# Spreading the attention row factors of a four-layer graph network by VectorE block transposes and DMA instead of TensorE transposes

## What is computed

```
x = layernorm(x + L0(x))      # 4 heads of 32: softmax(mask(q k^T / sqrt(32))) v, then @ wo.T + bo
x = layernorm(x + L1(x))      # h = x W; e[n,m] = leaky_relu(s1[n] + s2[m]); softmax over masked m; @ h
x = layernorm(x + L2(x))      # the same with 8 heads of 16 and a prior, then @ W_out.T
x = layernorm(x + L3(x))      # MLP, attention without mask, elu, MLP, masked attention, elu, residuals
```

## Time and profile before

| | us |
|---|---|
| median of 3 runs | 1141.66 |
| lowest, highest | 1140.52, 1142.09 |
| the profiled execution's own time | 1140.98 |
| its span, from the first to the last instruction | 1139.2 |
| PE busy (share of the span) | 1045.3 (92%) |
| DVE busy | 917.0 (80%) |
| ACT busy | 736.3 (65%) |
| POOL busy | 271.4 (24%) |

### The profile page before, as it was taken

The page is one execution under the profiler, slowest core; times in us unless marked ns, Lnnn a source line. Parts: engine busy times, 40 slices in busy tenths (PEclk is TensorE's granted clock), DMA queues, the critical chain, the costliest instruction groups (busy, mean ns, idle before and its releaser), DMA issues. The chain is left out here.

```text
span 1139.2 us, 26405 instructions
## 1 busy us (share of the span) xinstructions
PE 1045.3 (92%) x9333; PEld 782.5 (69%) x9333; DVE 917.0 (80%) x2514; ACT 736.3 (65%) x1901; POOL 271.4 (24%) x381
## 2 busy tenths in 40 slices
PE   2899999999999999999999999999999999879763
PEld 1567676877677767777787867777787768555552
DVE  4467999989897988979797997989797997977342
ACT  1699577757677684867678584867678584533522
POOL 0012212213131231413132141313132131421212
PEclk9999999999999999999999999999999999999877
DMA  4000000000000000000000000000000000000000
GB/s 120 1 11 12 11 2 11 1 11 11 10 2 12 10 11 11 11 11 11 11 2 11 10 11 11 11 11 11 11 1 11 2 11 2 10 1 10 10 0 19
DMA packets 9489, 12.97 MB, mean 11 GB/s; under 512 B 2704, under 2 KB 5008, under 8 KB 9232
## 3 DMA queue, kind: packets, MB, share of 16 engines
q1 hardware_dynamic: 9360, 11.28, 3.3%
HBM read 7.08 MB, written 4.19 MB: 10 GB/s over the span
## 5 line engine op out<-in xcount | busy, mean ns | idle before, releaser
L1119 DVE SCALAR_TENSOR_TENSOR P<-bank,t2e,mask_t 128x512 f32<-128x512 f32 x512 | 344.8, 739 | 19.1 <-PE bank L561 19.0
L703 ACT ACTIVATE probs<-probs,neg_max 128x512 f32<-128x512 f32 x256 | 184.8, 724 | 9.5 <-DVE neg_max L949 8.0
L748 ACT ACTIVATE x<-x,shift_l,rstd_l 128x128 f32<-128x128 f32 x256 | 105.6, 490 | 116.6 <-POOL shift_l L1252 116.4
L941 DVE CUSTOM_DVE_ANT_0 probs<-bank,mask_add 128x512 f32<-128x512 f32 x256 | 168.6, 677 | 15.3 <-PE bank L462 14.9
L713 ACT ACTIVATE probs_t<-bank 128x512 f32<-128x512 f32 x256 | 145.6, 614 | 10.4 <-PE bank L470 9.8
L470 PE MATMUL bank<-ident,probs 128*128 128x128 f32 x1024 | 139.6, 276 | 8.3 <-ACT probs_t L713 3.8
L470 PEld LDWEIGHTS bank<-ident,probs 128*128 128x128 f32 x1024 | 115.0, 141 | 28.9 <-ACT probs L703 15.2
L571 PE MATMUL bank<-P,GH 128*32 128x512 f32 x1024 | 119.7, 609 | 9.1 <-issue 8.2
L612 PE MATMUL bank<-t,l_P 128*128 128x257 f32 x512 | 121.2, 386 | 1.7 <-DVE l_P L1051 1.7
L612 PEld LDWEIGHTS bank<-t,l_P 128*128 128x128 f32 x512 | 94.6, 192 | 14.2 <-DVE l_P L1051 2.2
L571 PEld LDWEIGHTS bank<-P,GH 128*32 128x32 f32 x1024 | 32.2, 112 | 80.3 <-issue 78.9
(11 more groups left out here) (161 smaller groups left out, 1944.2 us busy)
## 6 DMA issues: line engine op xcount, KB each, us to landing
x_in<-in_x SPq DMA_DIRECT2D x16, 256.0 KB, 3.0
out<-x SPq DMA_DIRECT2D x16, 256.0 KB, 2.0
l_P<-in_adj SPq DMA_DIRECT2D x1, 1024.0 KB, 5.1
w_fc<-in_L_gnn_W_fc SPq DMA_DIRECT2D x1, 256.0 KB, 3.5
probs_t<-in_L_gnn_a_fc SPq DMA_DIRECT2D x1, 256.0 KB, 5.6
w_cat<-in_L_gnn_W SPq DMA_DIRECT2D x2, 64.0 KB, 3.6
w3a<-in_L_gnn_mlp_w SPq DMA_DIRECT2D x1, 128.0 KB, 3.8
w3b<-in_L_gnn_mlp_w SPq DMA_DIRECT2D x1, 128.0 KB, 3.3
```

The costliest lines, as they stand in the source:

```text
L703: act.activation(e, e, ACT.Exp, bias=neg_max[:, m:m + 1], scale=SCALE0, accum_out=g.of(den0)[:, m:m + 1])\
L748: last = act.activation(y[:, c, :], y[:, c, :], ACT.Identity, bias=shift[n][:, c:c + 1], scale=rstd[n][:, c:c + 1])
L941: dve.tensor_tensor_reduce(probs[c % 2][:, h, :], ps("l0_s", g, m)[:, :], mask_add[:, c, :], 1.0, -3.0e38, ALU.add, ALU.max, row_max[:, m: ...
L1119: last = dve.scalar_tensor_tensor(P2[:, h % GROUP2, j, :], ps("l2_s", g, h)[:, :], g.of(t2e)[:, j, h:h + 1], mask_t[:, j, :], ALU.max, ALU ...
```

## The change

The row factors no longer go through PE. After ACT has made R (or DVE the reciprocals), a new DVE stage `turn` transposes the 128x32 tile in blocks of 32x32 into `turned`, so that each block holds its 32 nodes along rows. SP then writes the four blocks with four DMAs into a small DRAM tensor `line` (`lay_out`, the `_rows` stages; 4 lines of 128 numbers, 16 for layer 0, 32 for layer 2), waits until they have landed, and reads a line of 512 numbers back into all 128 partitions of one of six row buffers `rows` (`spread`, the `_spread` stages, one DMA each; `l0_spread` is four DMAs of 32 partitions). `ROW_OF_USE` assigns the buffers, and a spread waits until the last reader of its buffer is done (`free_row`). The P stages and `l0_o` read the row buffer where they read a bank. `l0_rd`, `l1_s`, `l2_s`, `l3_s` and `l3b_s` are gone, and waits that hung on their banks hang on new semaphores. Each graph has five `turn` stages, five `_rows` and twelve `_spread` stages (eight for layer 2).

`x3` has a third buffer. Seven wide POOL instructions per graph (six of 512 columns and the minimum of 1024 columns in layer 3) are split into pieces of 128 columns, 32 in all. The orders of all engines and the bank assignment are new.

In the new order DVE runs, for example, `l0_rcp(8)`, `l2_o(5)`, `l0_turn(8)`, one `l2_p(6)`, `l3_turn(4)`, `l3b_turn(3)`, `l0_o(8)`, `l0_max(9)` twice, `l2_y(5)`, `l0_max(9)`, `l2_stats(5)`, `l3_p(4)`. SP runs at that place `l0_rows(8)`, `l0_spread(8)`, `l3_rows(4)`, `l3b_rows(3)`, `l2_spread(6)`, `l3_spread(4)`, `l3b_spread(3)`, two `l2_spread(6)`, `x_load(10)`, `l1_rows(8)`, `l1_spread(8)`, `l2_rows(7)`, four `l2_spread(7)`, `store(3)`. Between `l1_turn` and `l1_p`, `l2_turn` and the first `l2_p`, and `l3b_turn` and `l3b_p` there is more DVE work: `l2_dm`, `l3_z`, four `l0_max`, two `l3_zT`, `l3b_z` and small stages for layer 1; two `l0_max`, the `l1_p` and others for layer 2.

```diff
+ROWS = 6
+BLOCK = 32
...
-    "sp": "a:x_load d:store",
...
+    "sp": "a:x_load b:l0_rows c:l0_spread d:l1_rows e:l1_spread f:l2_rows g:l2_spread h:l3_rows i:l3_spread "
+          "j:l3b_rows k:l3b_spread l:store",
...
-        "a0a1a2a3a4a5a6d0a7d1a8d2a9d3aad4abd5acd6add7aed8afd9dadbdcdddedf",
...
+        "a6g2g2g2d4e4f3g3g3g3g3j0g3b5h1k0c5i1g3g3g3a7d5e5f4g4g4g4g4b6g4c6l0j1g4h2k1i2g4g4a8d6f5e6g5g5g5g5g5g5"
+        "b7l1c7h3g5j2i3k2g5a9d7e7f6g6g6g6g6l2g6b8c8h4j3g6i4k3g6g6aad8e8f7g7g7g7g7l3g7b9c9h5j4g7i5k4g7g7abd9e9"
+        "f8g8g8g8g8l4g8bacah6j5g8i6k5g8g8acdaeaf9g9g9g9l5g9g9bbcbh7j6g9i7k6g9g9addbebfagagagagal6gabccch8j7ga"
...
+ROW_OF_USE = (
...
+def row_uses():
+
+    used, transfers, last, at = {}, [0] * ROWS, [None] * ROWS, 0
+    for name, g, k in turns("sp"):
+        if name.endswith("_spread"):
+            r = int(ROW_OF_USE[at])
+            at += 1
+            transfers[r] += HEADS0 if name == "l0_spread" else 1
+            used[name, k, g.i] = r, transfers[r], last[r]
+            last[r] = name, k, g
+    return used
...
-        x1, x2, x3 = (pair(n, [P, C, D]) for n in ("x1", "x2", "x3"))
+        x1, x2, x3 = (pair(n, [P, C, D], n=k) for n, k in (("x1", 2), ("x2", 2), ("x3", 3)))
...
-        rden0 = sb("rden0", [P, 16])
+        rden0 = sb("rden0", [P, BLOCK])
+        turned0 = sb("turned0", [P, BLOCK])
...
+        rows = [sb(f"row{r}", [P, N_NODES]) for r in range(ROWS)]
...
+        line = {n: [nc.dram_tensor(f"{n}_line{q}", [parts * C, P], F32, kind="Internal").ap() for q in range(2)]
+                for n, parts in (("l0", HEADS0), ("l1", 1), ("l2", HEADS2), ("l3", 1), ("l3b", 1))}
...
+            def lay_out(n, turned, lines):
+                def f(g, k):
+                    sp.wait_ge(*sig(n + "_turned", g, 1))
+                    if n == "l0" and g.has(2):
+                        sp.wait_ge(*sig("o0_made", g, 1, back=2))
+                    for q in range(0, P, BLOCK):
+                        sp.dma_start(g.of(line[n])[:, q:q + BLOCK], turned[q:q + lines, :]).then_inc(signal[n + "_rows"], 16)
+                return f
+
+            def free_row(stage, g, k):
+                r, _, last = row_use[stage, k, g.i]
+                if last:
+                    sp.wait_ge(*row_read(last[0], last[2], last[1]))
+                return rows[r], row_filled[r]
+
+            def spread(n):
+                def f(g, k):
+                    if k == 0:
+                        sp.wait_ge(*sig(n + "_rows", g, 64))
+                    to, done = free_row(n + "_spread", g, k)
+                    sp.dma_start(to[:, :], g.of(line[n])[k * C:(k + 1) * C, :].rearrange("c p -> (c p)")
+                                 .rearrange("(o n) -> o n", o=1).broadcast_to([P, N_NODES])).then_inc(done, 16)
+                return f
+
+            def l0_spread(g, k):
+                sp.wait_ge(*sig("l0_rows", g, 64))
+                to, done = free_row("l0_spread", g, k)
+                for h in range(HEADS0):
+                    sp.dma_start(to[DH0 * h:DH0 * (h + 1), :], g.of(line["l0"])[h * C:(h + 1) * C, :].rearrange("c p -> (c p)")
+                                 .rearrange("(o n) -> o n", o=1).broadcast_to([DH0, N_NODES])).then_inc(done, 16)
...
-            def l0_rd(g, k):
-                pe.wait_ge(*sig("rden0_made", g, 1))
-                ps = empty("l0_rd", g)
-                for c in range(C):
-                    for h in range(HEADS0):
-                        m = HEADS0 * c + h
-                        last = pe.matmul(ps[DH0 * h:DH0 * (h + 1), c * P:(c + 1) * P],
-                                         rden0[:, m:m + 1].broadcast_to([P, DH0]), ident[:, :], start=True, stop=True)
-                last.then_inc(filled("l0_rd", g), 1)
...
-                pe.wait_ge(*took("l0_rd", g))
+                pe.wait_ge(*sig("o0_made", g, 1))
...
-            def spread_sources(n):
-                def f(g, k):
-                    pe.wait_ge(*sig(n + "_b", g, 3))
-                    ps = empty(n + "_s", g)
-                    for c in range(C):
-                        last = pe.transpose(ps[:, c * P:(c + 1) * P], gat[n]["R"][:, c:c + 1].broadcast_to([P, P]), ident[:, :])
-                    last.then_inc(filled(n + "_s", g), 1)
...
-                        pe.wait_ge(*took(n + "_s", g))
+                        pe.wait_ge(*sig(n + "_p", g, 1))
...
-            def l2_s(g, h):
-                if h == 0:
-                    pe.wait_ge(*sig("exp2", g, 3))
-                ps = empty("l2_s", g, h)
-                for c in range(C):
-                    last = pe.transpose(ps[:, c * P:(c + 1) * P], g.of(R2)[:, h, c:c + 1].broadcast_to([P, P]), ident[:, :])
-                last.then_inc(filled("l2_s", g, h), 1)
...
-                pe.wait_ge(*took("l2_s", g, GROUP2 * q + GROUP2 - 1))
+                pe.wait_ge(*sig("p2_made", g, GROUP2 * (q + 1)))
...
-                    dve.wait_ge(*wrote("l0_rd", g, back=1))
-                dve.reciprocal(rden0[:, :], g.of(den0)[:, :]).then_inc(signal["rden0_made"], 1)
+                    dve.wait_ge(*sig("l0_turned", g, 1, back=1))
+                dve.reciprocal(rden0[:, 0:HEADS0 * C].rearrange("p (h c) -> p c h", c=C), g.of(den0)[:, :].rearrange("p (c h) -> p c h", c=C)).then_inc(signal["rden0_made"], 1)
+            def turn(n, column, made, turned):
+
+                def f(g, k):
+                    dve.wait_ge(*made(g))
+                    if g.has(1):
+                        dve.wait_ge(*sig(n + "_rows", g, 64, back=1))
+                    dve.transpose(turned[:, :], column(g)).then_inc(signal[n + "_turned"], 1)
+                return f
...
-                dve.wait_ge(*wrote("l0_rd", g))
+                dve.wait_ge(*spread_done("l0_spread", g))
...
-                dve.tensor_tensor(o0_t[:, :], ps("l0_rd", g)[:, :], o0_raw[:, :], ALU.mult).then_inc(emptied("l0_rd", g), 1)
+                dve.tensor_tensor(o0_t[:, :], row("l0_spread", g)[:, :], o0_raw[:, :], ALU.mult).then_inc(signal["o0_made"], 1)
...
-                        dve.wait_ge(*wrote(n + "_s", g))
+                        dve.wait_ge(*spread_done(n + "_spread", g))
...
-                    made = dve.scalar_tensor_tensor(q["P"][:, j, :], ps(n + "_s", g)[:, :], q["b"][:, j:j + 1],
+                    made = dve.scalar_tensor_tensor(q["P"][:, j, :], row(n + "_spread", g)[:, :], q["b"][:, j:j + 1],
...
-                        made.then_inc(emptied(n + "_s", g), 1)
+                        made.then_inc(signal[n + "_p"], 1)
...
-                    made = dve.tensor_scalar(q["P"][:, j, :], ps(n + "_s", g)[:, :], q["g"][:, j:j + 1], q["b"][:, j:j + 1],
-                                             ALU.mult, ALU.max)
+                    made = dve.tensor_scalar(q["P"][:, j, :], row(n + "_spread", g)[:, :], q["g"][:, j:j + 1], q["b"][:, j:j + 1], ALU.mult, ALU.max)
...
-                dve.wait_ge(*wrote("l2_s", g, h))
+                dve.wait_ge(*spread_done("l2_spread", g, h))
...
-                    dve.wait_ge(*sig("l3_x", g, 1, back=2))
...
+                    dve.wait_ge(*sig("l3_x", g, 1, back=len(x3)))
...
-                pool.tensor_tensor(y[:, :, :], y[:, :, :], bias_o[:, :].unsqueeze(1).broadcast_to([P, C, D]), ALU.add)\
-                    .then_inc(signal["x_biased"], 1)
+                for c in range(C):
+                    last = pool.tensor_tensor(y[:, c, :], y[:, c, :], bias_o[:, :], ALU.add)
+                last.then_inc(signal["x_biased"], 1)
...
-                    pool.tensor_scalar(e[:, :, :], v(g)[:, :, :], 0.0, None, ALU.min).then_inc(signal[n + "_min"], 1)
+                    for c in range(C):
+                        for q in range(0, e.shape[2], P):
+                            last = pool.tensor_scalar(e[:, c, q:q + P], v(g)[:, c, q:q + P], 0.0, None, ALU.min)
+                    last.then_inc(signal[n + "_min"], 1)
```

301 lines of the change are left out of this document (167 added, 134 removed), and 16 rows, old and new, of the table STAGES.

## The result

The changed kernel takes 1183.65 us (median of 4 runs, 1182.88 to 1186.66) against 1141.22 us in the same session (1140.52 to 1142.09): ratio 1.0376, 95% interval 1.0356 to 1.0397. It is 42 us slower. I had predicted 1110, 1054 to 1155.

A forecast was written before the change was run, and what follows sets the result against it. PE was taken to bound the kernel, the bound then moving to DVE at 62.4 us per graph instead of 64.67. 1141.0 - 34 + 5 for the tail = 1112, given as 1110 us, range 1054 to 1155.

The forecast's parts named there:

- The sum: DVE per graph 56.5 + 3.0 + 2.9 = 62.4 us, above PE's 58.7, against 64.67 before: -34 us over 14.7 graphs.
- one term for the tail: At the end, the last l3b row trades 0.66 us of transposes for a 6.4 us trip: +5 us (0 to +12).
- PE's own work: Removing 44 transposes (4.8 us) and l0_rd (0.98 us) takes 5.8 us per graph off PE.
- the 93 that I had named as a sign: PE's busy time was to fall by about 93 us in all, to some 93% in the middle.
- Small terms of DVE: Per graph: P from SBUF 0, l3_p -0.75 us, five turns +0.75 us; DVE's own work stays 56.5 us.
- The port: DVE and POOL collide at one SBUF port, powers excepted: +3.0 us per graph for DVE, half of 6.0.
- The trip: DRAM round trip makes DVE wait before l0_o and l3_p: +2.9 us per graph, half of 5.8.
- The step that failed first: In the steady part PE, 98.3% busy, bounds the kernel; DVE has 8.1 us of slack per graph.
- The rivals of the port and of the trip: DVE pays the whole 6.0 us at SBUF: 1157 us, chance 0.13; l0_o and l3_p wait 5.8 us: 1155 us, 0.12.

The follow-up runs named there:

- e3: Changed kernel with each wide POOL instruction cut to 4 columns, the other columns left out: 1142.79 us, ratio 1.0047 to the kernel before.
- e2: Changed kernel with POOL's seven wide instructions per graph left whole instead of split: 1171.53 us, ratio 1.0276 to the kernel before.
- e4: New engine orders with the old transposes on PE, banks assigned anew, whole POOL instructions, three x3 buffers: 1213.16 us, ratio 1.0648 to the kernel before.
- e6: Kernel before with POOL's wide work cut to 4 columns, as a control: 1119.39 us, ratio 0.9812.
- e1: Changed kernel without row DMAs; spreads read input numbers and wait only for their buffer: 1137.99 us, ratio 0.9989 to the kernel before.
- e9: Kernel before with only a quarter of the transposes and matmuls that spread row factors on PE: 1131.30 us, ratio 0.9934.
- e5: Changed kernel without row DMAs and with POOL's wide work cut to 4 columns: 1098.21 us, ratio 0.9625 to the kernel before.

## Why the prediction was wrong

The sum made DVE the turn: its own work of 56.5 us, +3.0 at the port and +2.9 for the trip, with no other idle time, and added one term for the tail. Filling had no term. By the parts of the table at the top, it came out 73 us too low: 29 in the fifteen turns (-5.0 where I took -34; the middle turns measured 63.60 and not 62.4, the first three gained 1.2 us together and the last six lost 2.6), 40 in the filling, 2 at the end and 2 by rounding. That the turn came within 1.2 us of 62.4 is luck. DVE's own work was 55.7 us and not 59.5, its idle time 7.9 and not 2.9; the two errors nearly cancel.

- *PE's own work*: 5.8 us less per graph predicted; 63.5 fell to 0.921 x 63.60 = 58.5, 5.0 less. Right in the middle. Over the whole span PE's busy time fell by 61 us and not by the 93 that I had named as a sign.
- *Small terms of DVE*: P from SBUF at the same price is right (743 ns in e3 against 739); turns 0.2 us each, as taken. `l3_p` fell from 795 to 539 ns, 1.0 us per graph, where I took 0.75. The Trainium skill ("VectorE: DVE Perf Modes", the perf-mode tier table) says two elements a cycle for this fp32 instruction once its source is in SBUF; 539 ns is below the 607 of the row that I used (whose input is int32), so the trace agrees with the page's direction, if not with its full 1.07 us more.
- *The port*: +3.0 us per graph for DVE predicted, 0.6 measured with POOL's work in pieces (e3); with whole instructions (e2) it would be 32 x 0.038 + 4 x 0.172 = 1.9. The elu sum, from which I had read the collision, even fell from 1754 to 1235 ns; in e4, with whole POOL instructions, it is 1258, so it is the new order and not the pieces that shortened it. POOL paid instead: one of its 4-element instructions rose from 200 ns to 386 and the power from 1039 to 1212. It shows alone where both kernels have light POOL: the power takes 1034 ns in e6 and 1256 in e3, where P reads two inputs in SBUF. So my reading that the powers do not hold the port was wrong for this side of it: a power is held up by P. I had costed splitting at nothing ("shortens one wait, not their sum"); it costs 12 us (e2), and each piece takes more than its share of the whole.
- *The trip*: +2.9 predicted. `l0_o` waited 33.8 us and `l3_p` 9.5 in 700 us, (33.8 + 9.5)/11 = 3.9 us per graph, in the two places named. Without the trip (e1) `l0_o` still waits 20.7 us, 1.8 per graph, for ACT's `o0_raw`, so 2.1 us are the trip's, and the turn fell by 2.6. Mechanism and size were right, and so was the reason for taking half. Not seen was that it also costs some 11 of its 45.7 us in filling and end. A wait that I had not named, `l3_turn` for ACT's R, 15.9 us in 700, stays in e1 (16.7) and is not the trip's.
- *The step that failed first*: "DVE waits for PE 8.1 us per graph already", used as slack that the new loads could fill, and "PE bounds it", read from 98.3%. e9 shows that a lighter PE alone gives 7 us where I would have said 40 to 63, and e6 that PE is at 100.0% only without POOL's wide work. And of DVE's waits before, 85.8 us in 700 by the profile, only 43.5 were for PE, 4.0 per graph. DVE works 55.7 us of the new turn and waits 7.8, as it waited 7.9 before, but in other places: the waits of before (`l3_dmax` 18.4 us for ACT, `P` 16.5, `l3b_ndmax` 13.4 and `l3_rcp` 13.0 for PE) are gone or down to some 2 us each, and `l0_o` 33.8, `l3_turn` 15.9 and `l3_p` 9.5 stand in their place. The sum had let the idle time shrink to the trip's 2.9.
- *The step that was missing*, and the largest part of the miss: I priced the moved stages by what stands between a turn and its reader, and the new order itself at nothing. It keeps 1.4 graphs more in flight and runs 0.56 of a graph more before the first elu sum, and +37 us of filling is there even with trips and POOL free (e5 against e6). No run has the new order alone in a clean form (e4 has its own waits).

One way from the kernel before to the changed one: -21.2 us for relief and order without trips and wide POOL work (e6 to e5), +45.7 for the trips (e1), and for POOL 39.8 (e5 to e1) less the 21.5 that the kernel before pays too, +18.3. Together +42.8; measured, +42.4. Such a chain of runs closes by itself, so the sum proves nothing; what it gives is the size of each step. By the other way, over e3, the trips are 44.6 and POOL 40.9 less 21.5, so the sizes hold within some 2 us. The rivals of the port and of the trip had the right sign and each the wrong weight: the trip came in DVE's row at its forecast size and again in filling and end, and the port's cost came mostly in POOL's rows.

## What to carry to other kernels

An engine at 98% need not be alone at the bound. Idle time of another engine is not slack as a sum: look what each part of it waits for, and expect other waits in its place. The cheapest test is to make one engine lighter, with nothing moved, before building what relieves it. When a change needs a new order, count in the order how many units of work are in flight, and price the filling and the tail: here, with sixteen graphs and an order 1.4 graphs deeper, the start alone took 40 us more, eight times what the turns gained. Cutting a long instruction into pieces had only a price here, as nobody waited for its first piece: each stage signals after its last one.
